# A decoder layer on one core: ScalarE writes ALiBi's distances of two more head groups into the scores' banks

## The chip, the cores and the metric

The kernel runs on one core of one Trainium2 chip. The metric is the device time of one execution in microseconds (us); less is better. Before the change three executions took 542.37, 542.23 and 541.94 us, a median of 542.23 us. The spread of the three is 0.43 us.

The core's engines run their own instruction lists side by side and wait for each other by semaphores: PE (TensorE, matrix products, with its weight loads listed as PEld), ACT (ScalarE), DVE (VectorE), POOL (GpSimd) and SP (SyncE, which issues the DMAs). Products land in eight PSUM banks of 128 partitions by 512 float32.

## The reference, cut to what matters

One pre-norm decoder layer over x of 16 sequences, 128 tokens and 512 features: self attention with 16 heads of 32, cross attention over a context, and a gated feed-forward part whose weights are rounded to float8. The change touches only the self attention's scores:

```python
q = split(hidden_states @ Wq.T + bq)
k = split(hidden_states @ Wk.T + bk)
v = split(hidden_states @ Wv.T + bv)
scores = jnp.einsum('bhsd,bhtd->bhst', q, k)
rel = (pos[None, :] - pos[:, None]).astype(scores.dtype)
bias = alibi_slopes[:, None, None] * rel
scores = (scores + bias[None]) / math.sqrt(HD)
scores = 30.0 * jnp.tanh(scores / 30.0)
scores = jnp.where(causal[None, None], scores, -jnp.inf)
probs = jax.nn.softmax(scores, axis=-1)
ctx = jnp.einsum('bhst,bhtd->bhsd', probs, v)
...
x = x + attn(layernorm(x)); x = x + xattn(layernorm(x), ctx_2048, mask); x = x + ffn(layernorm(x))
```

`bias` is the head's slope times the distance between two tokens, the same for every sequence.

## The kernel before, in words

**Tiling.** The 16 sequences are four groups g of four sequences (GT = 4, 512 tokens), and the 16 heads are four head groups hg of four heads (HG = 4). Self attention goes through the 16 pairs (g, hg) in order; the feed-forward part follows. Each engine's list is written out by hand in this order, so what an engine does next never depends on times, only when it may begin does.

**One pair (g, hg) on TensorE.** First the scores of the four heads, one head j per bank, banks 2 to 5. Then the projections of the next head group's queries and keys (two times 12 products, banks 0 and 1, line 313), other work of the group (the values' projections at hg = 0; from g = 1 on the output projection `wo_proj` of the group before at hg = 1; transposes of the next group's tokens, `turn_x`, line 308, at hg = 2), and `context(g, hg)`: the sums of the probabilities (line 441) and the products with the values (line 451). The next scores follow at once.

**Two ways to get the bias into the scores.** `scores` issues four products (line 399, one a bank) of `bias_l` and `bias_r`, whose four rows hold slope and position in parts, and then adds the 16 products of keys and queries (line 410). `scores_onto` has no such products: it waits for the semaphore `seeded`, and its 16 products (line 425) are added onto what ScalarE has written into the four banks. `SEEDED` lists the pairs that go this way; before the change these are (1, 1), (1, 2), (2, 2) and (3, 2).

**The seed.** ScalarE's `seed(g, hg)` writes, for each j, slope times `distance` (token distances, one iota of GpSimd's, ready when `distance_made` is signalled) into bank 2 + j, line 1006. It needs that the bank's last scores were read, that is, that `tanh` of the pair before has run.

**One pair on ScalarE.** For each two heads `heads` runs `tanh` (line 992, from the bank) twice and `exp` (line 999) once; GpSimd then zeroes what lies above the diagonal (`causal`, line 820, signalled as `masked`), for which `context` waits. Then come `q_out` and `k_out` (lines 978 and 974), which copy the next head group's queries and keys out of banks 0 and 1 with their bias; the next scores need both. Behind them stand `context_high` (line 1021), the checks of rounded weight slabs (`flag_slabs`, lines 1031 and 1033, three instructions a slab), at hg = 0 the copies of the values (`v_out`, line 982), at hg = 2 the copies of the transposed tokens (`x_high`, line 969). VectorE forms the low parts and divides the context by its sums; it and GpSimd also round the weight slabs.

**What differs in group 0.** There is no output projection of a group before, so between the key projection of (0, 2) and the scores of (0, 2) TensorE has `context(0, 1)` alone.

Of the kernel before, what the change touches and what calls it, by code (L numbers as in the profile page):

```python
# [52 lines left out]
DOWN_FIRST = 8  # L53
W16_FIRST = 4

SEEDED = ((1, 1), (1, 2), (2, 2), (3, 2))

# [10 lines left out]
def slabs_at(table, g, hg):  # L70

    first = sum(map(sum, table[:g])) + sum(table[g][:hg])
    return range(first, first + table[g][hg])
# [6 lines left out]
def build(nc, x, memT, mem, mask, wT, small, bo, gate_w, up_w, down_w, down_s, out):  # L80
    quantized = nc.dram_tensor("quantized", [SLABS, P, 512], F32).ap()

    with ExitStack() as ctx:
# [179 lines left out]
        def wait_filled(e, item):  # L263
            b, n = seat[item]
            e.wait_ge(filled[b], n + 1)
            return bank[b]

        def wait_drained(e, item):
            b, n = seat[item]
            e.wait_ge(drained[b], n + 1)  # L270

        def drain_sem(item):
            return drained[seat[item][0]]
# [23 lines left out]
        def _(pe):  # L297
            def take(item, b):

                seat[item] = (b, seated[b])  # L300
                if seated[b]:
                    pe.wait_ge(drained[b], seated[b])
                seated[b] += 1
                return bank[b], filled[b]
# [109 lines left out]
            def scores_onto(g, hg):  # L414


                dst = [take(("S", g, hg, j), S_BANK + j) for j in range(4)]
                pe.wait_ge(seeded, (SEEDED.index((g, hg)) + 1) * 4)
                wait_drained(pe, ("Q", g, hg))
                wait_drained(pe, ("K", g, hg))  # L420
                for i in range(GT):
                    t = slice(i * S, (i + 1) * S)
                    for j in range(4):
                        rows = slice(HD * j, HD * (j + 1))
                        ins = pe.matmul(dst[j][0][:, t], kT[rows, t], qT[rows, t], start=False, stop=(i == GT - 1),  # L425
                                        skip_group_check=True)
                        if i == GT - 1:
                            ins.then_inc(dst[j][1], 1)
# [140 lines left out]
            for g in range(G):  # L569
# [13 lines left out]

                if (g, 1) in SEEDED:
                    scores_onto(g, 1)
# [8 lines left out]

                if (g, 2) in SEEDED:
                    scores_onto(g, 2)
# [362 lines left out]
        def _(act):  # L959
# [12 lines left out]
            def k_out(g, hg):  # L972
                src = wait_filled(act, ("K", g, hg))
                act.activation(kT[:], src[:], ACT.Identity, bias=bk_c[:, hg:hg + 1]).then_inc(drain_sem(("K", g, hg)), 1)

            def q_out(g, hg):
                src = wait_filled(act, ("Q", g, hg))
                act.activation(qT[:], src[:], ACT.Identity, bias=bq_c[:, hg:hg + 1]).then_inc(drain_sem(("Q", g, hg)), 1)

            def v_out(g, i):  # L980
                src = wait_filled(act, ("V", g, i))
                act.activation(v[:, i, :], src[:], ACT.Copy).then_inc(drain_sem(("V", g, i)), 1)
# [7 lines left out]
            def tanh(g, hg, j):  # L990
                src = wait_filled(act, ("S", g, hg, j))
                act.activation(probs[:, j].rearrange("p i s -> p (i s)"), src[:], ACT.Tanh,  # L992
                               scale=1.0 / (float(HD) ** 0.5 * CAP)).then_inc(drain_sem(("S", g, hg, j)), 1)

            def exp(g, hg, j):

                wait_drained(act, ("S", g, hg, j))
                wait_drained(act, ("S", g, hg, j + 1))
                act.activation(probs[:, j:j + 2], probs[:, j:j + 2], ACT.Exp, scale=CAP).then_inc(exped, 1)  # L999

            def seed(g, hg):
                if (g, hg) == SEEDED[0]:
                    act.wait_ge(distance_made, 1)
                for j in range(4):
                    wait_drained(act, ("S", g, hg - 1, j))
                    act.activation(bank[S_BANK + j][:].rearrange("p (i s) -> p i s", i=GT),
                                   distance[:].unsqueeze(1).to_broadcast([P, GT, S]), ACT.Copy,
                                   scale=slope_all[:, (hg - 1) * 4 + j:(hg - 1) * 4 + j + 1]).then_inc(seeded, 1)

            def heads(g, hg, j):  # L1010
                tanh(g, hg, j)
                tanh(g, hg, j + 1)
                exp(g, hg, j)
# [22 lines left out]
            def cross(g, k):  # L1036
                cross_first(g, k)
                cross_second(g, k)

            def cross_first(g, k):  # L1040
                if 0 <= k - 2 < GT:
                    i = k - 2
                    act.wait_ge(mem_loaded[i], 16 * (g + 1))
                    if i:

                        wait_filled(act, ("RO", g, i - 1))
                    elif g:

                        wait_filled(act, ("RO", g - 1, GT - 1))
                    act.activation(mem_hi[:], mem_sb[:, i, :], ACT.Copy).then_inc(mem_hi_made, 1)  # L1050
                    src = wait_filled(act, ("PT", g, i))
                    act.activation(x_pT_hi[:, i % 2, :], src[:, 0:S], ACT.Copy).then_inc(x_pT_hi_made, 1)

            def cross_second(g, k):
                if k == 1:

                    x2_out(g, k)
                if 0 <= k - 1 < GT:
                    n = (k - 1) % 2
                    act.wait_ge(xs_ready, g * GT + k)  # L1060
                    act.activation(x_sc[:, n, :], x_sc[:, n, :], ACT.Exp, bias=x_bias[:, n:n + 1],
                                   accum_out=x_den[:, n:n + 1]).then_inc(xs_exped, 1)
                if k < GT and k != 1:
                    x2_out(g, k)
# [28 lines left out]
            for g in range(G):  # L1093
                flagged = slabs_at(FLAGGED, g, 0)
                if g >= 2:
                    for j in range(4):
                        tanh(g, 0, j)
                    q_out(g, 1)
                    cross(g - 2, 2)
                    exp(g, 0, 0)  # L1100
                    k_out(g, 1)
                    cross_first(g - 2, 3)
                    exp(g, 0, 2)
                    cross_second(g - 2, 3)
                    cross_first(g - 2, 4)
                else:
                    heads(g, 0, 0)
                    heads(g, 0, 2)
                    q_out(g, 1)
                    k_out(g, 1)  # L1110
                if g == 1:
                    seed(g, 1)
                if g:
                    context_high(g - 1, 3)
                else:
                    weight_high(WO_PART)
                for i in range(GT):
                    if i < 3:
                        v_out(g, i)
                        if g >= 2 and i == 0:  # L1120
                            cross_second(g - 2, 4)
                        if g >= 2 and i == 1:
                            cross(g - 2, 5)
                        flag_slabs(flagged[i:i + 1 if i < 2 else None])
                    else:
                        v_out(g, i)

                heads(g, 1, 0)
                heads(g, 1, 2)
                q_out(g, 2)  # L1130
                k_out(g, 2)
                if g:
                    seed(g, 2)
                if g == 0:
                    context_high(g, 0)
                else:
                    norm_apply(g + 1)
                flag_slabs(slabs_at(FLAGGED, g, 1))
                if g:
                    context_high(g, 0)  # L1140

                heads(g, 2, 0)
                heads(g, 2, 2)
                q_out(g, 3)
                k_out(g, 3)
                for i in range(GT):
                    if i == 2:
                        context_high(g, 1)
                    x_high(g + 1, i)
                flag_slabs(slabs_at(FLAGGED, g, 2))  # L1150

                if g < G - 1:
                    heads(g, 3, 0)
                    heads(g, 3, 2)
                    q_out(g + 1, 0)
                    if g:
                        cross(g - 1, 0)
                    k_out(g + 1, 0)
                    if g:
                        cross(g - 1, 1)  # L1160
                    context_high(g, 2)
                    flag_slabs(slabs_at(FLAGGED, g, 3))
# [504 lines left out]
```

## Time and profile before

| what | value |
|---|---|
| executions timed | 541.94, 542.23, 542.37 us |
| profiled execution | 542.09 us, of which its span (first to last instruction) 540.4 us |
| TensorE busy | 535.2 us, 99% of the span |
| VectorE, ScalarE, GpSimd busy | 369.0, 287.9, 278.2 us (68%, 53%, 51%) |
| granted TensorE clock, mean over the span | 1.00 |
| DMA, mean | 103 GB/s |

The profile is one execution. Busy time of TensorE is modelled from pipelined products: two instructions that overlap count once, and a product that waits behind another counts as busy. So how long a stretch of TensorE takes is read from the starts of its weight loads and products, not from busy shares. The profiled execution's own time is 1.7 us longer than its span and 0.14 us shorter than the median.

### The profile page before, as it was taken

To read this page: it belongs to the slowest core of one execution; us is meant where nothing else is said; L and a number is where in the kernel's file an instruction comes from. 1 tells how busy PE (TensorE), PEld (TensorE's weight loads), DVE (VectorE), ACT (ScalarE), POOL (GpSimd) and SP (SyncE) were. 2 spreads that over 40 slices of the span, in tenths; PEclk is the share of its full clock that TensorE was granted. 3 is DMA by queue.
4 is the path that set the end of the run, shared out by engine and by line. 5 is a ranking of instruction groups with operands and counts; after the bars stand their busy time and mean duration, and the time that the engine had idled before them with its cause. 6 is when DMAs were issued, how large, how long until landed. Compare 5 with 4: busy or idle time off the path is not lost.

```text
span 540.4 us, 10126 instructions
## 1 busy us (share of the span) xinstructions
PE 535.2 (99%) x3918; PEld 424.0 (78%) x3918; DVE 369.0 (68%) x732; ACT 287.9 (53%) x514; POOL 278.2 (51%) x250
## 2 busy tenths in 40 slices
PE   8999999999999999999999999999999999999997
PEld 8888888888888888888888888684886758866686
DVE  7998958868566785678898988477533784253332
ACT  5958987978677785776753453036401363023310
POOL 5488698755773468576685349343300433013320
PEclk9999999999999999999999999999999999999999
DMA  8962222363216222039653715500510006100001
GB/s 300 333 215 72 79 92 66 103 213 118 79 41 200 74 59 61 21 127 283 215 216 108 263 34 113 148 0 1 107 52 36 1 1 137 39 21 0 1 19 58
DMA packets 62479, 55.46 MB, mean 103 GB/s; under 512 B 21472, under 2 KB 44256, under 8 KB 62432
## 3 DMA queue, kind: packets, MB, share of 16 engines
q1 hardware_dynamic: 62432, 54.82, 33.6%
q8 instruction: 31, 0.51, 0.4%
q14 instruction: 16, 0.13, 0.1%
HBM read 36.46 MB, written 13.63 MB: 93 GB/s over the span
## 4 chain that ended last, share of the span: by engine, by line
PE 99%; POOL 0%; DVE 0%; issue 0%; POOLq 0%
PE bank L313 45%; PE bank L522 24%; PE bank L538 15%; PE bank L441 3%; PE bank L451 3%; PE bank L308 2%; PE bank L410 2%; PE bank L362 1%; PE bank L561 1%; PE bank L549 1%; PE bank L399 1%; PE bank L425 1%; PE bank L467 0%; DVE y_sb L1555 0%; DVE y_sb L1557 0%
## 5 line engine op out<-in xcount | busy, mean ns | idle before, releaser
L313 PE MATMUL bank<-reduced 128*128 128x512 f32 x936 | 222.8, 394 | 0.1
L313 PEld LDWEIGHTS bank<-reduced 128*128 128x128 f32 x936 | 172.9, 188 | 37.5 <-issue 0.2
L927 POOL TENSOR_TENSOR f_parts<-fused,f_parts 128x512 fp32r<-128x512 f32 x48 | 62.3, 1298 | 147.0 <-ACT f_parts L1203 147.0
L1185 ACT ACTIVATE gate_parts<-bank,half_gate 128x512 f32<-128x512 f32 x48 | 33.0, 687 | 129.7 <-PE bank L522 121.6
L538 PE MATMUL bank<-reduced,f_parts 128*128 128x512 f32 x360 | 82.8, 390 | 0.0
L538 PEld LDWEIGHTS bank<-reduced,f_parts 128*128 128x128 f32 x360 | 67.4, 188 | 14.0
L522 PE MATMUL bank<-reduced 128*128 128x512 f32 x288 | 67.5, 393 | 0.0
L820 POOL TENSOR_SCALAR_AFFINE_SELECT probs<-probs 128x1024 f32<-128x1024 f32 x32 | 36.2, 1134 | 53.3 <-ACT probs L999 53.3
L522 PEld LDWEIGHTS bank<-reduced 128*128 128x128 f32 x288 | 54.1, 188 | 11.8
L1539 DVE SCALAR_TENSOR_TENSOR gate_parts<-gate_parts,bank 128x512 f32<-128x512 f32 x48 | 32.9, 686 | 42.6 <-ACT gate_parts L1185 42.6
L827 POOL TENSOR_TENSOR q_w<-q_w,q_m 128x512 f32<-128x512 f32 x36 | 53.0, 1473 | 17.2 <-DVE q_m L1368 17.2
L829 POOL TENSOR_TENSOR q_w<-q_w,q_m 128x512 f32<-128x512 f32 x36 | 48.1, 1336 | 2.8
L992 ACT ACTIVATE probs<-bank 128x512 f32<-128x512 f32 x64 | 34.2, 591 | 20.2 <-PE bank L410 14.0
L1567 DVE TENSOR_TENSOR y_sb<-bank,down_c 128x512 f32<-128x512 f32 x15 | 10.3, 689 | 49.1 <-PE bank L538 44.6
L522 PE MATMUL bank<-x,w_rest 128*128 128x512 f16 x192 | 42.0, 379 | 0.0
L1203 ACT ACTIVATE f_parts<-fused 128x512 fp32r<-128x512 f32 x48 | 30.0, 626 | 19.6 <-DVE fused L1546 19.3
L1546 DVE SCALAR_TENSOR_TENSOR fused<-bank,fuse_c,gate_parts 128x512 f32<-128x512 f32 x48 | 36.0, 751 | 4.1 <-PE bank L313 1.9
L522 PEld LDWEIGHTS bank<-x,w_rest 128*128 128x128 f16 x192 | 18.6, 98 | 22.7 <-issue 0.8
L999 ACT ACTIVATE probs<-probs 128x1024 f32<-128x1024 f32 x32 | 34.0, 1061 | 2.6
L1254 DVE BATCH_NORM_STATS2 bn<-x_res 128x6 f32<-128x512 f32 x48 | 31.4, 685 | 1.9 <-DMA x_res<-in_x 1.3
L1366 DVE TENSOR_SCALAR q_m<-q_w 128x512 uint32<-128x512 uint32 x36 | 27.9, 774 | 6.6 <-POOL q_w L829 6.1
L1368 DVE TENSOR_SCALAR q_m<-q_m 128x512 f32<-128x512 f32 x36 | 30.6, 850 | 1.2
(131 smaller groups left out, 748.3 us busy)
## 6 DMA issues: line engine op xcount, KB each, us to landing
quantized<-q_w SPq DMA_DIRECT2D x36, 256.0 KB, 3.4
reduced<-quantized SPq DMA_DIRECT2D x12, 512.0 KB, 7.3
memT_sb<-in_memT SPq DMA_DIRECT2D x16, 256.0 KB, 5.0
mem_sb<-in_mem SPq DMA_DIRECT2D x16, 256.0 KB, 5.7
out<-y_sb SPq DMA_DIRECT2D x15, 256.0 KB, 2.0
q_w<-in_gate_w SPq DMA_DIRECT2D x12, 256.0 KB, 3.3
q_w<-in_up_w SPq DMA_DIRECT2D x12, 256.0 KB, 3.2
x_res<-in_x SPq DMA_DIRECT2D x3, 1024.0 KB, 9.4
```

The source lines that it names most:

```text
L313: ins = pe.matmul(dst, stationary, moving, start=(n == 0), stop=(n == len(pairs) - 1))
L522: ins = pe.matmul(dst[:], stationary, moving, start=first and k == 0, stop=not first and k == KT - 1)
L538: ins = pe.matmul(dst[:], part[:, f, t], down_q[:, f], start=(f + n == 0), stop=(f + n == FT))
L820: pool.affine_select(out=two, in_=two, compare_op=ALU.is_ge, fill=0.0, base=0, pattern=[[0, 2 * GT], [1, S]], channel_multiplier=-1).then_ ...
L827: pool.tensor_tensor(w, w, m, ALU.add).then_inc(q_sum, 1)
L829: pool.tensor_tensor(w, w, m, ALU.subtract).then_inc(q_rounded, 1)
L927: pool.tensor_tensor(f_lo[:, f, :], fused[:, f % 2, :], f_hi[:, f, :].bitcast(F32), ALU.subtract).then_inc(f_lo_ready, 1)
L992: act.activation(probs[:, j].rearrange("p i s -> p (i s)"), src[:], ACT.Tanh, scale=1.0 / (float(HD) ** 0.5 * CAP)).then_inc(drain_sem(("S ...
L999: act.activation(probs[:, j:j + 2], probs[:, j:j + 2], ACT.Exp, scale=CAP).then_inc(exped, 1)
L1185: act.activation(tanh_g[:, f % 2, :], src[:], ACT.Tanh, scale=half_gate[:, f:f + 1]).then_inc(tanh_ready, 1)
L1539: dve.scalar_tensor_tensor(silu2[:, f % 2, :], tanh_g[:, f % 2, :], 1.0, bank[gates][:], ALU.add, ALU.mult)\
L1546: dve.scalar_tensor_tensor(fused[:, f % 2, :], ups[:], fuse_c[:, f:f + 1], silu2[:, f % 2, :], ALU.mult, ALU.mult).then_inc(drain_sem(("U" ...
```

## The change

Two pairs are added to `SEEDED`, (0, 1) and (0, 2). TensorE takes `scores_onto` for them. ScalarE writes their seeds at these places: for (0, 1) the banks of heads 0 and 1 behind `v_out(0, 0)` and those of heads 2 and 3 behind `v_out(0, 1)`; for (0, 2) all four behind `k_out(0, 2)`, where the other groups have theirs. The wait for `distance_made` moves with the first seed.

```diff
-SEEDED = ((1, 1), (1, 2), (2, 2), (3, 2))
+SEEDED = ((0, 1), (0, 2), (1, 1), (1, 2), (2, 2), (3, 2))
...
-            def seed(g, hg):
-                if (g, hg) == SEEDED[0]:
+            def seed(g, hg, heads=range(4)):
+                if (g, hg) == SEEDED[0] and 0 in heads:
                     act.wait_ge(distance_made, 1)
-                for j in range(4):
+                for j in heads:
                     wait_drained(act, ("S", g, hg - 1, j))
...
                     if i < 3:
                         v_out(g, i)
+                        if g == 0 and i < 2:
+                            seed(0, 1, (2 * i, 2 * i + 1))
...
                 q_out(g, 2)
                 k_out(g, 2)
-                if g:
-                    seed(g, 2)
+                seed(g, 2)
                 if g == 0:
                     context_high(g, 0)
```

On TensorE, the scores of (0, 2), with the waits of each row (drained0 and drained1 are the banks of queries and keys, drained2 to drained5 those of the scores):

```order
 L451 MATMUL bank<-probs,v 32x128 x16
-L399 MATMUL bank<-bias_r,bias_l 128x512 [waits drained4,drained5,drained3,drained2]
-L399 MATMUL bank<-bias_r,bias_l 128x512 x3
-L410 MATMUL bank<-qT,kT 128x128 [waits drained1,drained0]
-L410 MATMUL bank<-qT,kT 128x128 x15
+L425 MATMUL bank<-qT,kT 128x128 [waits seeded,drained5,drained0,drained4,drained1,drained3,drained2]
+L425 MATMUL bank<-qT,kT 128x128 x15
 L313 MATMUL bank<-reduced 128x512 [waits drained5,w_lo_made,drained4,drained0,drained3,drained2]
```

The four products of the bias are gone, and the first product of keys and queries also waits for `seeded`. The scores of (0, 1) change in the same way.

On ScalarE, behind the projections of the values of group 0 (filled6 and filled7 are the banks of the first two):

```order
 L982 ACTIVATE v<-bank 128x512 [waits filled6]
+L1006 ACTIVATE bank<-place_n,small_c 128x512 [waits drained2,distance_made]
+L1006 ACTIVATE bank<-place_n,small_c 128x512 [waits drained3]
 L1031 ACTIVATE q_j<-q_w 128x512 [waits q_rounded]
 L1033 ACTIVATE q_j,flags<-q_j 128x512 [waits q_over]
 L982 ACTIVATE v<-bank 128x512 [waits filled7]
+L1006 ACTIVATE bank<-place_n,small_c 128x512 [waits drained4]
+L1006 ACTIVATE bank<-place_n,small_c 128x512 [waits drained5]
 L1031 ACTIVATE q_j<-q_w 128x512 [waits q_rounded]
```

Two seeds now stand ahead of each of the first two slabs' checks.

On ScalarE, behind the queries and keys of (0, 2):

```order
 L978 ACTIVATE qT<-bank,small_c 128x512 [waits filled0]
 L974 ACTIVATE kT<-bank,small_c 128x512 [waits filled1]
+L1006 ACTIVATE bank<-place_n,small_c 128x512 [waits drained2]
+L1006 ACTIVATE bank<-place_n,small_c 128x512 [waits drained3]
+L1006 ACTIVATE bank<-place_n,small_c 128x512 [waits drained4]
+L1006 ACTIVATE bank<-place_n,small_c 128x512 [waits drained5]
 L1021 ACTIVATE reduced<-ctxT,small_c 128x512 [waits drained6]
 L1031 ACTIVATE q_j<-q_w 128x512 [waits q_rounded]
```

Four seeds stand between the keys' copy and `context_high(0, 0)`, the slab's check and the `tanh` of (0, 2).

## Rows read from the trace of the kernel before

**Rows 1.** The page: busy time of each engine, and the chain that ended last.
```profile
PE 535.2 (99%) x3918; PEld 424.0 (78%) x3918; DVE 369.0 (68%) x732; ACT 287.9 (53%) x514; POOL 278.2 (51%) x250
...
PE 99%; POOL 0%; DVE 0%; issue 0%; POOLq 0%
```

**Rows 2.** Timeline of PE's weight loads: start us, us, engine, line, count [idle before].
```profile
43.03 0.92 PEld L451 LDWEIGHTS bank<-probs,v 128*32 128x32 f32 x32
44.15 0.19 PEld L399 LDWEIGHTS bank<-bias_r,bias_l 4*128 4x128 f32 x4 [0.20 <-issue]
44.26 1.10 PEld L410 LDWEIGHTS bank<-qT,kT 32*128 32x128 f32 x32
45.48 5.31 PEld L313 LDWEIGHTS bank<-reduced 128*128 128x128 f32 x24
...
83.10 0.98 PEld L425 LDWEIGHTS bank<-qT,kT 32*128 32x128 f32 x32 [0.20 <-issue]
84.21 16.23 PEld L313 LDWEIGHTS bank<-reduced 128*128 128x128 f32 x72
...
102.68 0.98 PEld L425 LDWEIGHTS bank<-qT,kT 32*128 32x128 f32 x32 [0.20 <-issue]
```

**Rows 3.** Timeline of PE's products from the projections of (0, 2) to context(0, 2).
```profile
36.49 5.74 PE L313 MATMUL bank<-reduced 128*128 128x512 f32 x24
42.27 1.08 PE L441 MATMUL bank<-probs,sums_to 128*32 128x128 f32 x32
...
45.48 5.74 PE L313 MATMUL bank<-reduced 128*128 128x512 f32 x24
51.05 1.49 PE L308 MATMUL bank<-identity,xn_r 128*128 128x128 f32 x16
52.47 1.08 PE L441 MATMUL bank<-probs,sums_to 128*32 128x128 f32 x32
```

**Rows 4.** Timeline of ACT around the first two values of group 0.
```profile
25.23 0.60 ACT L982 ACTIVATE v<-bank 128x512 f32<-128x512 f32 x1 [0.22 <-PE bank L313]
26.13 0.63 ACT L1031 ACTIVATE q_j<-q_w 128x512 f32<-128x512 f32 x1 [0.30 <-POOL q_w L829]
...
27.95 0.60 ACT L982 ACTIVATE v<-bank 128x512 f32<-128x512 f32 x1 [0.42 <-PE bank L313]
30.86 0.64 ACT L1031 ACTIVATE q_j<-q_w 128x512 f32<-128x512 f32 x1 [2.31 <-POOL q_w L829]
```

**Rows 5.** Timeline of ACT from the queries of (0, 2) to the first tanh of (0, 2).
```profile
40.86 0.67 ACT L978 ACTIVATE qT<-bank,small_c 128x512 f32<-128x512 f32 x1
42.27 0.69 ACT L974 ACTIVATE kT<-bank,small_c 128x512 f32<-128x512 f32 x1 [0.74 <-PE bank L313]
42.85 0.71 ACT L1021 ACTIVATE reduced<-ctxT,small_c 128x512 fp32r<-128x512 f32 x1
43.47 0.62 ACT L1031 ACTIVATE q_j<-q_w 128x512 f32<-128x512 f32 x1
...
45.57 1.09 ACT L992 ACTIVATE probs<-bank 128x512 f32<-128x512 f32 x2 [0.73 <-PE bank L410]
```

**Rows 6.** Timeline of ACT, one of the four seeds of before with what follows it.
```profile
90.61 2.52 ACT L1006 ACTIVATE bank<-place_n,small_c 128x512 f32<-128x512 f32 x4
93.06 2.93 ACT L987 ACTIVATE xn<-x_res,shift,rstd 128x512 f32<-128x512 f32 x4
...
103.87 1.09 ACT L992 ACTIVATE probs<-bank 128x512 f32<-128x512 f32 x2 [0.88 <-PE bank L425]
```

**Rows 7.** Timeline of POOL: the distances, and the second mask of (0, 2).
```profile
18.08 0.24 POOL L877 IOTA place_n<- 128x128 f32 x1 [6.84 <-DVE bias_r L1404]
...
50.00 1.25 POOL L820 TENSOR_SCALAR_AFFINE_SELECT probs<-probs 128x1024 f32<-128x1024 f32 x1 [0.85 <-ACT probs L999]
```

**Rows 8.** Timeline of ACT from the queries of (0, 3) to the first tanh of (0, 3).
```profile
49.84 0.67 ACT L978 ACTIVATE qT<-bank,small_c 128x512 f32<-128x512 f32 x1
51.25 0.69 ACT L974 ACTIVATE kT<-bank,small_c 128x512 f32<-128x512 f32 x1 [0.74 <-PE bank L313]
...
54.36 0.66 ACT L1031 ACTIVATE q_j<-q_w 128x512 f32<-128x512 f32 x1
...
55.78 1.09 ACT L992 ACTIVATE probs<-bank 128x512 f32<-128x512 f32 x2
```

**Rows 9.** Waits of PEld (us, times, longest); the first and a later turn_x on PE.
```profile
PEld bank L308 <- ACT probs L992: 0.5, 2, 0.3
...
6.30 0.78 PE L308 MATMUL bank<-identity,xn_r 128*128 128x128 f32 x4
...
9.24 0.46 PE L308 MATMUL bank<-identity,xn_r 128*128 128x128 f32 x4
```

## The prediction

> **What bounds the kernel now.** I read the page's busy times first: TensorE is busy for 99% of the span, and the chain that ended last is TensorE for 99% of it [rows 1]. So every microsecond that TensorE's list gets shorter, or stands still, shows in the end one for one, unless it stood still at that moment anyway. Next I listed who waited for whom: behind its start TensorE hardly waits for another engine; the largest entry of its weight loads for one is 0.5 us in two places [rows 9]. There is next to no idle time on it in which a new wait could hide. Then I took the timeline at the two places of the change, TensorE and ScalarE side by side. Two things are to be seen: what the four bias products cost there, and how close behind the keys' copy the scores of (0, 2) begin.
>
> **What is removed.** With bias products the stretch from the first weight load of the scores to the first of the next projection is 44.15 to 45.48, 1.33 us; without them, in the pair (1, 1) that was seeded already, it is 83.10 to 84.21, 1.11 us [rows 2]. The loads of the four have only 0.11 us to themselves, and the rest of the saving is that the first keys' product no longer stands behind a 512-column one. Both stretches are from this kernel, at one clock. So a removed set is worth 0.22 us (1.33 less 1.11), and two are worth 0.44 us.
>
> **The seeds of (0, 1).** A set of four seeds takes 2.52 us on ScalarE, and the next instruction starts 2.45 us after the first [rows 6]. The two behind the first value start at about 25.73 (the copy starts at 25.23) and hold the slab's check back from 26.13 to 26.95, and through it the copy of the second value from 27.95 to about 28.35 [rows 4]; the bank it frees is wanted by context(0, 0), some 5 us later. The next two run until about 30.1, ahead of the 30.86 at which the second slab is rounded: ScalarE had waited 2.31 us for that [rows 4]. From 30.86 on all is as before. The distances are made at 18.08 to 18.32 [rows 7], so the moved wait costs nothing. The scores of (0, 1) stand behind context(0, 0) and find their banks seeded by 5 us. Cost nothing, gain 0.22 us; from there on TensorE, and ScalarE which waits for it, are 0.22 us ahead. If the cover were gone, a stall of at most those four seeds' 2.45 us would follow; with 5 us of room I put no weight on it.
>
> **The seeds of (0, 2).** Here the new wait bites. The seeds stand behind the keys' copy, and this copy waits for TensorE's own last projection product: ScalarE sat idle for 0.74 us and began at 42.27, right as the 24 products ended (36.49 plus 5.74 is 42.23) [rows 3, 5]. The next instruction can start 0.58 us later (42.85) [rows 5]. With the 0.22 us gained, the first seed starts at 42.63 and the last ends 2.52 us later, at 45.15. TensorE has only context(0, 1) in between, and comes to the scores at 44.15 less 0.22, at 43.93 [rows 2]. In groups 1 to 3 the output projection lies between; here nothing does. For the release I take 0.05 us, near the 0.04 us between 42.23 and 42.27 the other way. So TensorE stands still from 43.93 to 45.20, 1.27 us. The seeded scores take 1.11 us, the next projection starts at 46.31, where it started at 45.48: 0.83 us later. As a sum: -0.22 -0.22 +1.27 = +0.83 us.
> That price has two ends. If the seeds went as one and the release were free it would be 1.22 us of standing; if the wait also kept the four first weight loads from overlapping and the release took 0.15 us, about 1.45. So +0.78 to +1.01.
>
> **What is late next.** ScalarE has more behind it than TensorE: context_high, a slab's check, then tanh of (0, 2). context_high starts at 42.63 plus 2.45, 45.08; the check 0.62 us later (42.85 to 43.47) [rows 5]; tanh 1.42 us behind that (54.36 to 55.78) [rows 8]: 47.12, against 45.57 before [rows 5]. The scores are there earlier, at 45.20 plus 1.19 (102.68 to 103.87) [rows 2, 6], 46.39. So ScalarE is late by 1.55 us, more than TensorE. What absorbs the difference is that it waited for TensorE before the next keys' copy, 0.74 us [rows 8]: the queries' copy now starts at 49.84 plus 1.55, 51.39; ScalarE is free for the keys at about 52.0; the keys are there at 46.31 plus 5.74 plus 0.04, 52.09. It meets its data with 0.09 us to spare, and from here both engines are late by the same 0.83 us. The second mask of (0, 2) ran from 50.00 to 51.25 [rows 7]; late by 1.55 it ends at 52.80, and context(0, 2) wants it at 52.47 plus 0.83, 53.30 [rows 3]: half a microsecond to spare. The fourth group of turn_x, which needs the keys' bank, moves with the keys' copy. VectorE and GpSimd follow those two engines here, and DMAs only gain time. After that every pair is as before, 0.83 us later, to the end.
>
> **The sum.** The profiled execution took 542.09 us, so 542.92; against the median of 542.23, 0.14 us higher, it is 543.06. I predict 543.1 us, 0.15% above before. About 0.2% (1.08 us; below 541.15 or above 543.31) is what a measurement of this kernel can tell from no change.
>
> **Rivals.**
> First, slower than that bound: ScalarE's lateness is not absorbed. It has 0.09 us to spare at the keys of (0, 3). Each further 0.1 us there (a longer check of the slab, a seed slowed by TensorE writing other banks) goes on to TensorE, since turn_x waits for the keys' bank, context for the mask and the next scores for the keys. It decides from 0.1 us on. At most all of the 1.55 us stays: 542.23 plus 1.55, 543.8; a half of the difference gives 543.4. For it: the margin is thin. Against it: the 16 seeds of before and the copies are steady to some hundredths, and a second idle time of ScalarE's lay before the tanh in most pairs. 0.17.
> Second, the delay is given back in part: TensorE's few waits later (0.5 us in two places [rows 9]) are for ScalarE, which could have caught up. Against it: ScalarE in turn waits for TensorE's scores in each pair. 542.23 plus 0.83 less at most 0.5: 542.6. 0.08.
> Third, the seeds are in time, or the wait costs nothing: only the saving is left, 542.23 less 0.44, 541.8. That would need ScalarE to have written four banks in the 1.3 us between the keys' copy's second half and the scores; rows 5 and 6 exclude it. 0.03.
> Fourth, the clock. TensorE stands still for 1.27 us, longer than at any time after its start. What a lower granted clock costs can be seen at the start: four transposes took 0.78 us at 6.30 and 0.46 us at 9.24 [rows 9]. If the next 24 projection products (5.74 us [rows 3]) ran at half speed, 5.7 us would be added: 548.8. The Trainium skill (TensorE: Matmul & The Clock Gate, "What's actually happening") says that TensorE goes back to 1.2 GHz after idling and regains 2.4 GHz by sustained work; in this trace the slow transposes are the ones right after TensorE's first idle time, which agrees in kind, and no row shows a fall after a gap as short as this one. 0.02.
> The forecast itself has 0.70; its own range is 542.9 to 543.3.
>
> **How the numbers follow.** The forecast and the second and third rivals lie within 0.2%: 0.81 in sum; but the forecast's upper end touches the bound at 543.31, and run to run the medians move by 0.2 us, so I move 0.07 of it over. Slower: 0.17 plus 0.02 plus 0.07, 0.26. Faster: 0.01, for a seeding cheaper than any row shows. Same: 0.73. The range reaches down to the second rival less the runs' spread and up to the first rival's end: 542.4 to 543.9.
>
> **What would show it.** In the changed kernel's profile: the first weight load of line 425 at 83 to 84 us will be the third of its kind; the first two should start near 35.2 and near 45.2, the second with about 1.3 us of idle before it that ends with ScalarE's line 1006; the seeds of (0, 2) from 42.6 to 45.2; from the second start to the next line 313 about 1.11 us; tanh of (0, 2) at 47.1 without a wait; the keys' copy of (0, 3) at 52.1 with almost no idle before it; context(0, 2) at 53.3; the rest 0.8 us late. I am wrong if line 425's second start is before 44.5 or if the shift at 80 us differs from the one at 46 us. A granted clock below 1.00 would show the fourth.

## The result, and the profile after

| | executions | median us (lowest to highest) |
|---|---|---|
| before | 14 | 542.36 (541.94 to 543.56) |
| changed | 14 | 543.22 (542.92 to 543.79) |

The ratio is 1.0015, with a 95% interval of 1.0008 to 1.0022. The kernel became 0.86 us slower by the medians: below the 0.2% that I had called no change, but outside the measurement's own interval. The forecast was 543.1 us, 0.83 us above before. In a second set, beside other kernels, the changed kernel took 543.14 us against 542.37, a ratio of 1.0014 (1.0005 to 1.0023).

The profiled execution took 543.26 us, its span is 541.5. The first part of the profile's page and the head of its chain, which answer to [rows 1]:

```profile
PE 534.8 (99%) x3910; PEld 423.7 (78%) x3910; DVE 368.3 (68%) x732; ACT 292.5 (54%) x522; POOL 278.9 (51%) x250
...
PE 98%; ACT 1%; POOL 0%; DVE 0%; issue 0%; POOLq 0%
```

TensorE has eight products fewer and is busy 0.4 us less, ScalarE has eight instructions and 4.6 us more, and ScalarE now has its 1% of the chain that ended last. That 1% is one place. The timeline of TensorE's weight loads, from context(0, 0) on, answers to [rows 2]:

```profile
33.49 0.81 PEld L441 LDWEIGHTS bank<-probs,sums_to 128*32 128x32 f32 x32 [0.35 <-issue]
...
35.37 0.98 PEld L425 LDWEIGHTS bank<-qT,kT 32*128 32x128 f32 x32 [0.20 <-issue]
36.48 5.35 PEld L313 LDWEIGHTS bank<-reduced 128*128 128x128 f32 x24
42.33 0.84 PEld L441 LDWEIGHTS bank<-probs,sums_to 128*32 128x32 f32 x32 [0.50 <-issue]
...
45.72 1.01 PEld L425 LDWEIGHTS bank<-qT,kT 32*128 32x128 f32 x32 [1.68 <-issue]
46.85 5.31 PEld L313 LDWEIGHTS bank<-reduced 128*128 128x128 f32 x24
```

The scores of (0, 1) take 1.11 us instead of 1.33, without a wait. Those of (0, 2) begin behind 1.68 us of idle time where the other seeded pairs have 0.20. Who ended it is in the chain that ended last, cut to this place (start, length, what):

```profile
42.27 0.02 issue
42.29 0.69 ACT kT L974
42.98 2.42 ACT bank L1006 x4
45.40 0.35 issue
45.75 1.17 PE bank L425 x32
```

The path leaves TensorE at the keys' copy, goes through the four seeds, and comes back 0.35 us after the last one (0.33 us from that seed's end, 45.39, to the first weight load, 45.72). In the kernel before, TensorE's context(0, 1) stood there. ScalarE's timeline, which answers to [rows 5, 8]:

```profile
42.29 0.69 ACT L974 ACTIVATE kT<-bank,small_c 128x512 f32<-128x512 f32 x1 [0.79 <-PE bank L313]
42.88 2.51 ACT L1006 ACTIVATE bank<-place_n,small_c 128x512 f32<-128x512 f32 x4
45.33 0.71 ACT L1021 ACTIVATE reduced<-ctxT,small_c 128x512 fp32r<-128x512 f32 x1
...
47.22 1.07 ACT L992 ACTIVATE probs<-bank 128x512 f32<-128x512 f32 x2
...
51.47 0.67 ACT L978 ACTIVATE qT<-bank,small_c 128x512 f32<-128x512 f32 x1
52.63 0.69 ACT L974 ACTIVATE kT<-bank,small_c 128x512 f32<-128x512 f32 x1 [0.49 <-PE bank L313]
```

The tanh of (0, 2) starts without a wait at 47.22 (forecast 47.1), and the keys' copy of (0, 3) still finds 0.49 us of idle time before it.

**How traces are compared below.** The span's start moves: context(0, 0) began at 33.28 us in the kernel before and between 33.16 and 33.68 in the others, with the same instructions ahead of it. So I count from there. Before:

```profile
33.28 0.81 PEld L441 LDWEIGHTS bank<-probs,sums_to 128*32 128x32 f32 x32 [0.35 <-issue]
...
55.68 2.41 PEld L313 LDWEIGHTS bank<-reduced 128*128 128x128 f32 x11
```

Two stretches matter. A is from that point to the projection behind the scores of (0, 2): 45.48 less 33.28, 12.20 us before; 46.85 less 33.49, 13.36 us changed. B is to the first product behind the scores of (0, 3): 55.68 less 33.28, 22.40 us before; 57.06 less 33.49, 23.57 us changed. Both are 1.16 to 1.17 us longer: nothing more is lost and nothing given back between them.

### The profile page after: what moved, and what is told of

The parts are those of the page before. It is cut to its first block, busy times and chain, and to the rows that moved or that the text cites. A ratio compares the mean times of both kernels' runs of the same rounds, so it can differ in the third digit from the quotient of the medians.

```text
span 541.5 us, 10118 instructions
## 1 busy us (share of the span) xinstructions
PE 534.8 (99%) x3910; PEld 423.7 (78%) x3910; DVE 368.3 (68%) x732; ACT 292.5 (54%) x522; POOL 278.9 (51%) x250
## 4 chain that ended last, share of the span: by engine, by line
PE 98%; ACT 1%; POOL 0%; DVE 0%; issue 0%; POOLq 0%
PE bank L313 45%; PE bank L522 24%; PE bank L538 15%; PE bank L441 3%; PE bank L451 2%; PE bank L308 2%; PE bank L410 2%; PE bank L425 1%; PE bank L362 1%; PE bank L561 1%; PE bank L549 1%; PE bank L399 1%; ACT bank L1006 0%; PE bank L467 0%; ACT kT L974 0%
## 5 line engine op out<-in xcount | busy, mean ns | idle before, releaser
L829 POOL TENSOR_TENSOR q_w<-q_w,q_m 128x512 f32<-128x512 f32 x36 | 48.2, 1339 | 2.8
```

The costliest lines, as they stand in the source:

```text
L829: pool.tensor_tensor(w, w, m, ALU.subtract).then_inc(q_rounded, 1)
```

## The experiments

Each ran beside the kernel before on one chip; e1 to e4 share one set of it; e7, e9, r_changed and the repeat of e3 another; e5, e6 and the repeats of e1 and e9 a third.

| kernel | A | B | time, us | before, us | ratio (95%) |
|---|---|---|---|---|---|
| before | 12.20 | 22.40 | | | |
| changed, again (r_changed) | 13.36 | 23.58 | 543.14 | 542.37 | 1.0014 (1.0005 to 1.0023) |
| e1, (0, 1) alone | 12.08 | 22.30 | 542.04 | 542.25 | 0.9999 (0.9990 to 1.0008) |
| the same again | 12.39 | 22.60 | 541.88 | 542.17 | 0.9996 (0.9987 to 1.0005) |
| e2, (0, 2) alone | 13.55 | 23.85 | 543.30 | 542.25 | 1.0021 (1.0012 to 1.0030) |
| e3, one wait | 13.06 | 23.27 | 543.26 | 542.25 | 1.0017 (1.0008 to 1.0026) |
| the same again | 13.05 | 23.26 | 543.11 | 542.37 | 1.0012 (1.0003 to 1.0021) |
| e4, one seed ahead | 12.75 | 23.00 | 542.76 | 542.25 | 1.0009 (1.0000 to 1.0018) |
| e7, both | 12.45 | 22.95 | 542.57 | 542.37 | 1.0004 (0.9995 to 1.0013) |
| e5, seeds twice | 16.74 | 28.37 | 547.51 | 542.17 | 1.0099 (1.0085 to 1.0113) |
| e6, ScalarE late only | 12.13 | 23.38 | 542.96 | 542.17 | 1.0016 (1.0007 to 1.0024) |
| e9, seeds on VectorE | 11.73 | 21.94 | 541.84 | 542.37 | 1.0001 (0.9986 to 1.0016) |
| the same again | 11.93 | 22.14 | 541.74 | 542.17 | 0.9992 (0.9983 to 1.0000) |

**Half of the change each: e1 and e2.**

```diff
 e1
+SEEDED = ((0, 1), (1, 1), (1, 2), (2, 2), (3, 2))
+                if g:
+                    seed(g, 2)
 e2
+SEEDED = ((0, 2), (1, 1), (1, 2), (2, 2), (3, 2))
-                        if g == 0 and i < 2:
-                            seed(0, 1, (2 * i, 2 * i + 1))
```

> Only the pair (0, 1) is added to the seeded ones; (0, 2) keeps its four bias products and has no seeds. Theory A (the loss is TensorE standing still for the seeds of (0, 2), 1.48 us in the changed kernel's trace): no wait at the scores of (0, 2), which begin 0.1 to 0.25 us earlier than before; time 0.1 to 0.2 us below the kernel before, near 542.2. Theory B (six seeded pairs cost ScalarE or the slabs more than they give, wherever they stand): half of the loss stays, +0.4 us, near 542.8.

> Only the pair (0, 2) is added; (0, 1) keeps its bias products. Theory A: the whole loss is here, and the gain of (0, 1) is missing: TensorE waits 1.4 to 1.5 us before the scores of (0, 2), time 1.0 to 1.2 us above the kernel before, near 543.5. Theory B: half of the loss, +0.4 us, near 542.8.

> The kernel in which only (0, 1) is added, once more beside the others. Its profile was 0.1 us ahead at the projection behind (0, 2) and 0.4 us at the end, counted from context(0, 0). Time 0.1 to 0.3 us below the kernel before, and 0.2 to 0.3 us above the one with VectorE's seeds.

Theory A holds. With (0, 2) alone the loss is all there and more, +1.05 us in time and +1.35 in stretch A; with (0, 1) alone nothing is lost, and both sets lie 0.2 to 0.3 us below before, which neither interval can tell from none. The gain of (0, 1) is not sure to last: in the repeat, stretch A was 12.39, longer than before. The wait behind it is for the mask. GpSimd's second mask of (0, 1) in its timeline, in e1 and then in its repeat:

```profile
40.93 1.22 POOL L820 TENSOR_SCALAR_AFFINE_SELECT probs<-probs 128x1024 f32<-128x1024 f32 x1 [0.80 <-ACT probs L999]
```
```profile
40.74 1.52 POOL L820 TENSOR_SCALAR_AFFINE_SELECT probs<-probs 128x1024 f32<-128x1024 f32 x1 [0.96 <-ACT probs L999]
```

The same instruction took 1.09 us in the profile before. In e1 and its repeat it ended at 42.15 and 42.26, and context(0, 1) began 0.11 us behind it both times, at 42.26 and 42.37. So here GpSimd's mask, not TensorE, sets when context(0, 1) begins.

**The release: e3 and its repeat.** ScalarE's seeds stand behind its reads of the banks and behind the copies of queries and keys, so whoever has waited for the seeds need not wait for the six others.

```diff
-                dst = [take(("S", g, hg, j), S_BANK + j) for j in range(4)]
+                dst = [take(("S", g, hg, j), S_BANK + j, False) for j in range(4)]
                 pe.wait_ge(seeded, (SEEDED.index((g, hg)) + 1) * 4)
-                wait_drained(pe, ("Q", g, hg))
-                wait_drained(pe, ("K", g, hg))
...
-                if seated[b]:
+                if seated[b] and wait:
                     pe.wait_ge(drained[b], seated[b])
```

> As changed, but scores_onto waits for the seeds alone. ScalarE writes them behind its reads of the four banks and behind the copies of queries and keys, so the six other waits are held by this one. In the changed kernel's trace 0.33 us pass between the end of the last seed (45.39) and the first weight load (45.72), with three wait instructions in between, 0.11 us apart, the first of them the one for the seeds. Theory A1 (these are walked through only after the seeds are signalled): the first weight load comes 0.05 to 0.12 us behind the last seed, the wait of TensorE is 0.2 to 0.28 us shorter and the time 0.2 to 0.28 us below the changed kernel, near 543.0. Theory A2 (the time between is ScalarE's write reaching the bank): still 0.3 us, time as changed, near 543.2.

> The kernel in which scores_onto waits for the seeds alone, once more beside the changed kernel. Its profile showed the shorter release (shift of the projection behind the scores of (0, 2): +0.97 us against +1.38), its time did not (543.26 us). Theory A1: time 0.2 to 0.3 us below the changed kernel of this set. Rival: the time saved is given back somewhere in most executions; no difference.

A1 holds, in the profile. The chain that ended last, in e3 (its lines are numbered two less):

```profile
42.88 2.42 ACT bank L1004 x4
45.30 0.04 issue
45.34 1.17 PE bank L423 x32
```

0.04 us instead of 0.35 from the last seed to TensorE. In the changed kernel the first of three wait instructions holds for the seeds, and the other two and the weight load are walked through only then. Stretches A and B are 0.30 to 0.32 us shorter in both profiles. The time is not: 543.26 and 543.11 us against the changed kernel's 543.22 and 543.14. The profiles show where much of the saving goes. The weight loads of context(0, 3) and the first of the scores behind it, in the changed kernel and in e3's repeat:

```profile
62.80 0.84 PEld L441 LDWEIGHTS bank<-probs,sums_to 128*32 128x32 f32 x32 [0.37 <-issue]
...
64.72 0.19 PEld L399 LDWEIGHTS bank<-bias_r,bias_l 4*128 4x128 f32 x4 [0.20 <-issue]
```
```profile
62.37 0.91 PEld L439 LDWEIGHTS bank<-probs,sums_to 128*32 128x32 f32 x31 [0.37 <-issue]
...
64.46 0.19 PEld L399 LDWEIGHTS bank<-bias_r,bias_l 4*128 4x128 f32 x4 [0.20 <-issue]
```

The stretch takes 1.92 us in both profiles of the changed kernel, and 2.04 and 2.09 us in e3 and its repeat. No row shows a wait in it; why it is longer stays open. At the last weight load of the span the lead of e3 over the changed kernel is down to 0.14 us, and that of the repeats to 0.10 us, which is no more than chance moves such medians.

**One seed into ScalarE's idle time: e4, and with the one wait: e7.**

```diff
                 q_out(g, 2)
+                if g == 0:
+                    seed(g, 2, (0,))
                 k_out(g, 2)
-                seed(g, 2)
+                seed(g, 2, (1, 2, 3) if g == 0 else range(4))
```

> As changed, but the first of the four seeds of (0, 2) stands ahead of the copy of the keys, in the 0.79 us that ScalarE waits there. TensorE's wait before the scores of (0, 2) gets 0.61 us shorter (0.85 to 0.9 us instead of 1.48). If only that wait counts, time 0.6 us below the changed kernel, near 542.6. If ScalarE's own lateness (tanh of (0, 2) begins at 46.6 at the earliest, with the same work behind it) takes over at the next keys' copy, where 0.49 us of idle time are left in the changed kernel, the rest is held there. ScalarE too comes to that work 0.61 us earlier, so I expect the full 0.6 us; a gain of 0.3 or less would say that something else holds it.

> Both edits: one seed ahead of the keys' copy, and scores_onto waits for the seeds alone. If they add up, TensorE's wait is 1.48 less 0.61 less 0.28, 0.6 us, and the time 0.75 to 0.9 us below the changed kernel, near 542.4, about the kernel before. If ScalarE's lateness holds the rest, the idle time before the keys' copy of (0, 3) is used up (0.54 us with one ahead) and the time stays near 542.7.

e4 gave what one seed takes: stretches A and B are 0.6 us shorter, the time 0.46 us below the first changed median (the lead at the last weight load is 0.43 us) and 0.5 us above before. So the seeds behind the keys' copy are on the path, one for one. e7 came out between its two cases. Stretch A is 0.91 us shorter (12.45), as if the two added up, but B only 0.63. Between the last products of context(0, 2) and the scores of (0, 3) the weight loads of e7 show what took it:

```profile
53.66 0.90 PEld L449 LDWEIGHTS bank<-probs,v 128*32 128x32 f32 x32
55.02 0.22 PEld L399 LDWEIGHTS bank<-bias_r,bias_l 4*128 4x128 f32 x4 [0.46 <-issue]
```

From the first of these rows to the second it is 1.36 us, where the changed kernel has 1.09 (54.64 to 55.73). Those scores need banks 2 and 3, which VectorE frees, and VectorE was late:

```profile
52.35 1.40 DVE L1369 TENSOR_SCALAR q_m<-q_m 128x512 f32<-128x512 f32 x1
53.67 2.47 DVE L1273 TENSOR_TENSOR reduced<-bank,reduced 128x512 fp32r<-128x512 f32 x4
```

Its first low part (line 1273) ran straight behind the preparation of a slab, without idle time; in the repeat of the changed kernel VectorE had waited 2.50 us for ScalarE before the same instruction:

```profile
53.81 1.29 DVE L1273 TENSOR_TENSOR reduced<-bank,reduced 128x512 fp32r<-128x512 f32 x2 [2.50 <-ACT reduced L969]
```

With TensorE earlier, the third engine in the row became the bound.

**Twice the seeds: e5.** ScalarE writes the four seeds of (0, 2) a second time, each behind its first, and TensorE waits for the second four.

```diff
                     wait_drained(act, ("S", g, hg - 1, j))
+                    if twice:
+                        act.wait_ge(seeded, 4 + j + 1)
...
                 seed(g, 2)
+                if g == 0:
+                    seed(g, 2, twice=True)
...
-                pe.wait_ge(seeded, (SEEDED.index((g, hg)) + 1) * 4)
+                pe.wait_ge(seeded, (SEEDED.index((g, hg)) + 1) * 4 + (4 if (g, hg) != (0, 1) else 0))
```

> As changed, but ScalarE writes the four seeds of (0, 2) twice, and TensorE waits for the second four. If each us of ScalarE between the keys' copy and the scores costs one us: TensorE stands still 2.5 us longer (1.4 plus 2.5, about 3.9 us), time near 545.7, granted clock 1.00. If a gap of nearly 4 us lowers the clock, the projection products behind it (24 in 5.7 us in the changed kernel) take longer, up to twice as long, and the time is above 547.

The second case came true: the clock fell. TensorE's products in e5:

```profile
48.04 2.09 PE L425 MATMUL bank<-qT,kT 32*128 32x128 f32 x32 [3.99 <-ACT bank L1008]
50.07 7.17 PE L313 MATMUL bank<-reduced 128*128 128x512 f32 x24
57.07 1.49 PE L308 MATMUL bank<-identity,xn_r 128*128 128x128 f32 x16
```

and its busy times by stretch (length, busy of PE, PEld, DVE, ACT and POOL, then the granted clock, the DMA share and GB/s):

```profile
44.00:49.00 5.00, 1.01 (x20) 0.99 (x20) 3.42 (x4) 4.97 (x10) 3.50 (x3) 0.73 0.00 2
49.00:51.00 2.00, 2.00 (x26) 1.67 (x19) 1.92 (x11) 1.48 (x4) 0.00 (x0) 0.50 0.32 74
51.00:54.00 3.00, 3.00 (x10) 2.32 (x9) 1.43 (x3) 2.82 (x5) 1.09 (x1) 0.64 0.35 125
54.00:60.00 6.00, 6.00 (x87) 5.33 (x89) 1.29 (x2) 3.90 (x8) 4.89 (x4) 1.00 0.01 4
```

After 3.99 us without a product the granted clock is 0.50 (1.2 GHz), and TensorE has it back in full before 54. The scores took 2.09 us instead of 1.17 and the projection 7.17 instead of 5.74, 2.4 us in all. The median of its four executions (547.0 to 548.1 us) is 4.3 us above the changed kernel. Stretch B has 4.8 us more than there: 2.45 for ScalarE's four further seeds and 2.35 for the clock. In the changed kernel the time without a product was 1.44 us, and the stretch behind it still has the full clock (TensorE's timeline, and the busy times by stretch, of the changed kernel):

```profile
45.75 1.17 PE L425 MATMUL bank<-qT,kT 32*128 32x128 f32 x32 [1.44 <-ACT bank L1006]
```
```profile
46.00:52.00 6.00, 6.00 (x55) 5.00 (x52) 4.94 (x13) 5.79 (x11) 3.79 (x4) 1.00 0.28 87
```

The Trainium skill (TensorE: Matmul & The Clock Gate, "What's actually happening") has TensorE fall to 1.2 GHz when it idles for long and come back by sustained work. The trace of e5 agrees, with 0.50 behind a gap of 3.99 us and 1.00 again from 54 us on; the changed kernel's 1.44 us brought no fall.

**Lateness by itself: e6.**

```diff
+                    if g == 0 and i == 0:
+                        act.wait_ge(aside, 4)
... (on top of e1's "if g:")
+                else:
+                    for j in range(4):
+                        if j:
+                            act.wait_ge(aside, j)
+                        act.activation(mem_hi[:].rearrange("p (i s) -> p i s", i=GT),
+                                       distance[:].unsqueeze(1).to_broadcast([P, GT, S]), ACT.Copy,
+                                       scale=slope_all[:, 4 + j:5 + j]).then_inc(aside, 1)
```

> Only (0, 1) is seeded; at the place of the four seeds of (0, 2) ScalarE writes four times into an SBUF tile that nobody reads then, each behind the one before. TensorE does not wait for them at the scores of (0, 2). It leaves out nothing. It tells what ScalarE's lateness costs by itself. Theory A (my prediction's second step: the lateness is held by the 0.74 us that ScalarE idles before the keys' copy of (0, 3), and costs only because TensorE does not wait beforehand): tanh of (0, 2) starts 2 us late, near 47.6, the keys' copy of (0, 3) near 52.6 without idle time before it, 1.2 to 1.4 us late, and TensorE waits that long there; time 1.1 to 1.4 us above the kernel with (0, 1) alone, near 543.3. Theory B (only a wait at the scores costs, ScalarE's other work has room): as the kernel with (0, 1) alone, 542.1.

Theory A holds in kind. At the scores of (0, 2) TensorE loses nothing (A is 12.13), and it loses 1.1 us further on (B is 23.38, against 22.30 in e1), where it waits for the copies of queries and keys:

```profile
PEld bank L309 <- ACT qT L979: 0.8, 1, 0.8
...
PEld bank L309 <- ACT kT L975: 0.2, 1, 0.2
```

The time is 1.08 us above that of e1's repeat on the same chip, and less than 0.3 us below the changed kernel's. So four such writes in ScalarE's list between the keys of (0, 2) and the tanh of (0, 2) cost TensorE about 1 us even when it doesn't wait for them. But they are longer than the seeds, since each waits for the one before:

```profile
43.07 2.98 ACT L1143 ACTIVATE mem_hi<-place_n,small_c 128x512 fp32r<-128x512 f32 x4
45.95 0.71 ACT L1022 ACTIVATE reduced<-ctxT,small_c 128x512 fp32r<-128x512 f32 x1
```

The next instruction starts 2.88 us behind the first write, and 2.45 us behind the first seed in the changed kernel. ScalarE has no idle time from here to its copies for (0, 3), so the 0.43 us too much go on to TensorE. For writes as short as the seeds the loss in B would be 1.08 less 0.43, about 0.65 us: an estimate. That is half of the 1.27 us by which the changed kernel's B is longer than e1's. So the lateness of ScalarE alone costs about half, and a kernel without the wait would have won about the other half; no run shows this with the seeds' own length.

**The seeds on another engine: e9 and its repeat.**

```diff
                     norm_apply(0, 1, 1)
+                    dve.wait_ge(distance_made, 1)
+                    for j in range(4):
+                        wait_drained(dve, ("S", 0, 1, j))
+                        dve.tensor_scalar(bank[S_BANK + j][:].rearrange("p (i s) -> p i s", i=GT),
+                                          distance[:].unsqueeze(1).to_broadcast([P, GT, S]),
+                                          slope_all[:, 4 + j:5 + j], None, ALU.mult).then_inc(vector_seeded, 1)
-                    prepare_slabs(slabs)
+                    prepare_slabs(slabs[:1])
...
-                seed(g, 2)
+                if g:
+                    seed(g, 2)
...
                 normalize_context(g, 1)
+                if g == 0:
+                    prepare_slabs(slabs_at(PREPARED, 0, 1)[1:])
...
-                pe.wait_ge(seeded, (SEEDED.index((g, hg)) + 1) * 4)
+                if (g, hg) == (0, 2):
+                    pe.wait_ge(vector_seeded, 4)
+                else:
+                    pe.wait_ge(seeded, (SEEDED.index((g, hg)) + 1 - (g > 0)) * 4)
```

> As changed, but VectorE writes the four seeds of (0, 2), behind its norm_apply(0, 1, 1), which ended at 40.7; the preparation of one slab moves behind normalize_context(0, 1). ScalarE has no seeds there. If VectorE writes a seed in 0.6 to 0.7 us, the four end by 43.3, ahead of the scores of (0, 2) at 43.9, TensorE does not wait, and both savings of 0.22 us are left: time 0.3 to 0.45 us below the kernel before, near 541.9. If VectorE is slowed there as in its other operations between 42 and 45 us (1.3 to 1.5 us instead of 0.4), the seeds end after 45 and the time is at least that of the changed kernel, 543.2 or more.

> The kernel whose (0, 2) is seeded by VectorE, once more, since one of its 11 executions took 546.04 us and three others over 542.4. Median 541.7 to 541.9, 0.4 to 0.5 us below the kernel before. If the long executions belong to it, they come again in about a third of them; if they were chance, its spread is that of the others here.

The seeds took VectorE 2.70 us from 40.52 on (its timeline), and the scores of (0, 2) began with the idle time of the other seeded pairs (the timeline of the weight loads, here lines 429 and 314):

```profile
40.52 2.70 DVE L1480 TENSOR_SCALAR bank<-place_n,small_c 128x512 f32<-128x512 f32 x4
```
```profile
43.79 0.98 PEld L429 LDWEIGHTS bank<-qT,kT 32*128 32x128 f32 x32 [0.20 <-issue]
44.89 1.23 PEld L314 LDWEIGHTS bank<-reduced 128*128 128x128 f32 x6
```

Stretch A is 11.73, 0.47 us shorter than before: the two savings of 0.22 us, both kept. In the repeat GpSimd's second mask of (0, 1) took 1.28 us, and A is 11.93, only 0.27 us shorter. The edit also moves the preparation of a slab; what that does by itself was not run. The medians are 0.53 and 0.43 us below before in two sets, with lowest times of 541.37 in both. In the first set one of 11 executions took 546.04 us, which widens its interval; none of the repeat was above 542.8. The repeat's interval ends at 1.0000, so that this version beats the kernel before by 0.08% is likely and not proven. Against the changed kernel its gain is clear: 1.3 us between the medians of one set (1.5 between the repeat and the first changed median), and the repeat's interval lies wholly below the changed kernel's two.

**The base again.**

> The changed kernel once more, on the same chip as the others of this set, as their base. 543.1 to 543.3 us. In the first profile TensorE came 0.1 us late to context(0, 1) although the scores of (0, 1) had gained 0.22 us; if that is the mask's length on GpSimd (1.22 us against 1.09 before) and no rule, it should lie elsewhere between 0 and 0.1 us here.

Stretches A and B came out as in the first profile to 0.01 us. The mask took 1.31 us here, and context(0, 1) kept only 0.01 us of the 0.22; but TensorE's idle time before the scores of (0, 2) was 1.58 us and not 1.68. What the mask takes from TensorE there, the wait for the seeds gives back.

## Why the prediction was right, step by step

- **What bounds the kernel, and what a removed set of bias products is worth.** Right: 0.22 us each. e9, where nothing is waited for, is 0.47 us shorter in A.
- **The seeds of (0, 1) cost nothing.** Right that they cost nothing: ScalarE's second slab check still waited 0.83 us for its slab, behind all four seeds. But that their gain reaches the rest of the chain was too simple. Before, the mask had ended at 42.12 and context(0, 1) began at 42.23, so TensorE was already waiting for GpSimd there, by less than 0.1 us, which I had not seen; in the changed kernel the mask took 1.22 us instead of 1.09 and context(0, 1) kept 0.11 us of the 0.22.
- **The seeds of (0, 2).** The mechanism, its place and the seeds' times are as forecast (42.63 to 45.15; measured 42.88 to 45.39, of which 0.21 us is the later start of context(0, 0)). The term for the release was mis-sized: I took 0.05 us, with 0.15 as its end, and it was 0.33. I had taken it from the start of ScalarE's keys' copy behind TensorE's last product; here three wait instructions and a load come behind each other. e3 showed it: with one wait it is 0.04 to 0.05.
- **The sum.** -0.22 and -0.22 and +1.27 were forecast, +0.83. The profile has -0.22 for the scores of (0, 1), +0.11 for the mask, +1.47 for the wait (45.72 less the 44.25 at which context(0, 1) ends by its old length) and -0.20 for the scores of (0, 2): +1.16, and so is stretch A. Of the 0.33 us between +0.83 and +1.16, 0.28 are the release, 0.04 the start of the first seed (42.67 when counted from context(0, 0), forecast 42.63) and 0.02 the scores. The mask's 0.11 us is not among them, since the wait shrank by it.
- **The rest as before, to the end.** Wrong by 0.2 to 0.3 us, and here the number had luck. The time has +0.86 and +0.77, less than the profile's +1.16 at the end of B. The kernel before has an idle time of 0.37 us before a cross-attention product at 207.84, which none of the other kernels' profiles has. Ahead of it stands VectorE's line 1339, in the kernel before and then (line 1340) in the changed one:

```profile
205.16 1.84 DVE L1339 TENSOR_TENSOR mem_lo<-mem_sb,mem_hi 128x512 fp32r<-128x512 f32 x1 [0.18 <-ACT mem_hi L1050]
```
```profile
206.31 1.11 DVE L1340 TENSOR_TENSOR mem_lo<-mem_sb,mem_hi 128x512 fp32r<-128x512 f32 x1
```

  VectorE's next three operations end at 207.72 before and 208.14 changed, and TensorE needs the last of them. From there on the changed kernel is behind by 0.93 us, and its repeat by 0.87, counted from context(0, 0) to the last weight load; that is near the timed +0.86 and +0.77. Of the other eleven profiles, nine agree in the same way with their timed differences to within 0.22 us (not the repeat of e1, nor e5). One profile of the kernel before can't tell whether it always stops there. The release was forecast 0.28 us too short and this was not forecast at all; that 543.1 came so close to 543.22 is owed to the two cancelling.
- **What is late next.** Right: tanh of (0, 2) at 47.22 and without a wait, and ScalarE's lateness held by the idle time before the keys of (0, 3). The margin was 0.49 us and not 0.09, since TensorE was later than forecast and the slab's check took 1.28 us and not 1.42. e6 shows that this second path is a real one; with the seeds' own length it is worth about 0.65 us by the estimate there, half of the first.
- **The rivals.** ScalarE's lateness kept on: not here, but e6 is that case, at +0.79 us. Given back in part: 0.2 to 0.3 us of the profile's loss were, at 207.84 us and by VectorE, not by ScalarE as I had it. The saving alone: only by another engine (e9). The clock: not after 1.44 us, but after 3.99 us (e5); the 5.7 us that I had put on it were too much, it was 2.4 in e5.

## What to carry to other kernels

Work taken off a saturated engine is a gain only where the engine that takes it over is not the next in the same chain: look at what lies between the data's arrival and the consumer, and count each instruction put there at its full length. Where the wait goes away, count again what is queued behind the moved work: here that second path alone would still have cost about half (the estimate from e6). If a third engine has room at that moment, give the work to it.

A wait that decides should be alone, or last: conditions that it implies cost time behind it, 0.1 us for each further wait instruction in the profiles here. That this shortens the whole kernel was not shown (e3's time did not fall).

A difference of a few tenths is not settled at the place of the change: compare the traces to the last instruction, too.

## What the runs showed of the hardware

- From the end of the last seed to TensorE's first weight load: 0.33 us with seven conditions in three wait instructions and the load, 0.04 to 0.05 us with one.
- A seed, 128x512 float32 from SBUF into a bank with a scale per partition, took ScalarE 0.68 us (0.61 us apart) and VectorE 0.74 us (0.65 apart) in both of e9's profiles. VectorE's next operation (line 1372) was not as steady: 1.40 us at 43.14 and 0.42 us at 48.14 in e9.
- After 3.99 us without a product the granted clock stood at 0.50, and products were slower for some 5 us; after 1.44 us it did not move.
- GpSimd's mask of 128x1024, the second of (0, 1), took between 1.09 us (the kernel before, e2, e4, e7, e9 and the repeat of e3) and 1.52 us (the repeat of e1). What slows it is not settled.
